# Row maxima of attention scores: five two-bank reduces per head in place of twelve one-bank ones

## The reference

```python
k = (x @ Wk).reshape(B, H, T, hs)      # B 32, H 6, T 1024, hs 16
q = (x @ Wq).reshape(B, H, T, hs)
v = (x @ Wv).reshape(B, H, T, hs)
wei = einsum('bhtd,bhsd->bhts', q, k) * C ** -0.5
wei = where(tril(ones((T, T))), wei, -inf)
wei = softmax(wei, axis=-1)
out = einsum('bhts,bhsd->bhtd', wei, v).reshape(B, T, C)
return out @ Wp + bp
```

## Time and profile before

| | us |
|---|---|
| median of 3 runs | 2901.9 |
| lowest, highest run | 2897.7, 2904.84 |
| profiled execution, span from first to last instruction | 2901.5 |

### The profile page before, as it was taken

How to read it: one execution, slowest core, us unless ns; L and a number is a source line. 1 busy time by engine, 2 the same in 40 slices (tenths; PEclk the granted TensorE clock), 3 DMA queues, 4 the chain that set the end, 5 groups by cost and what they waited for, 6 DMA issues and landing times. The chain is left out here.

```text
span 2901.5 us, 86028 instructions
## 1 busy us (share of the span) xinstructions
PE 2730.6 (94%) x28924; PEld 1685.7 (58%) x29306; DVE 2300.3 (79%) x4585; ACT 2020.8 (70%) x3943; POOL 1153.0 (40%) x1999
## 2 busy tenths in 40 slices
PE   4999999999999499999999999999999997899996
PEld 2555555555554266666666666666666664455553
DVE  3577676676765499999999999999999994678997
ACT  2677777777776267777777777777777774577775
POOL 1144443444434434444444444444444441224445
PEclk9999999999999699999999999999999998999998
DMA  1113223232332466666666666666666663334555
GB/s 34 44 55 115 90 100 114 76 114 85 105 114 85 128 118 119 116 118 118 118 118 118 118 118 118 118 117 117 117 117 117 118 117 86 99 105 132 147 142 154
DMA packets 923408, 316.04 MB, mean 109 GB/s; under 512 B 848785, under 2 KB 906418, under 8 KB 923314
## 3 DMA queue, kind: packets, MB, share of 16 engines
q1 hardware_dynamic: 921970, 313.59, 47.8%
q10 hardware_dynamic: 1344, 1.18, 0.1%
HBM read 113.35 MB, written 99.88 MB: 73 GB/s over the span
## 5 line engine op out<-in xcount | busy, mean ns | idle before, releaser
L982 DVE TENSOR_REDUCE at_unit_max<-at_ps_queries 128x1 f32<-128x512 f32 (+4 forms) x2304 | 1135.9, 550 | 86.0 <-PE at_ps_queries L853 83.5
L928 ACT ACTIVATE at_probs<-at_ps_keys 128x512 f32<-128x512 f32 x1344 | 743.3, 603 | 388.9 <-PE at_ps_keys L868 384.5
L853 PE MATMUL at_ps_queries<-at_turned 96*128 96x128 bf16 (+3 forms) x3456 | 635.1, 275 | 30.6 <-DMA at_turned<-at_spread 29.4
L868 PE MATMUL at_ps_keys<-at_turned 128*128 128x128 bf16 x3453 | 648.4, 275 | 13.3 <-ACT at_probs L928 1.7
L803 POOL TENSOR_TENSOR at_v<-at_stacks,at_one 128x128 f32<-128x128 f32 x192 | 76.7, 399 | 818.5 <-DMA at_stacks<-qkv_rows 818.5
L888 PE MATMUL at_ps_values<-at_probs,at_v 128*32 128x128 f32 x10752 | 373.4, 276 | 6.5 <-ACT at_probs L928 6.5
L868 PEld LDWEIGHTS at_ps_keys<-at_turned 128*128 128x128 bf16 x3456 | 238.0, 97 | 239.5 <-ACT at_probs L928 88.3
L853 PEld LDWEIGHTS at_ps_queries<-at_turned 96*128 96x128 bf16 x3456 | 289.7, 98 | 122.0 <-DMA at_turned<-at_spread 31.3
L888 PEld LDWEIGHTS at_ps_values<-at_probs,at_v 128*32 128x32 f32 x10752 | 269.5, 109 | 120.6 <-ACT at_diag_probs L928 70.2
L928 ACT ACTIVATE at_diag_probs<-at_ps_keys 128x512 f32<-128x512 f32 x384 | 208.7, 595 | 8.5 <-PE at_ps_keys L868 5.6
L822 POOL TENSOR_SCALAR_AFFINE_SELECT at_diag_probs<-at_diag_probs 128x1024 f32<-128x1024 f32 x192 | 210.3, 1095 | 0.0
(11 more groups left out here) (214 smaller groups left out, 4967.4 us busy)
## 6 DMA issues: line engine op xcount, KB each, us to landing
qkv_rows<-cb_packed SPq DMA_DIRECT2D x32, 1536.0 KB, 8.3
at_stacks<-qkv_rows SPq DMA_DIRECT2D x192, 256.0 KB, 3.3
cb_x<-in_x_dram SPq DMA_DIRECT2D x32, 384.0 KB, 3.7
cb_x_again<-in_x_dram SPq DMA_DIRECT2D x32, 384.0 KB, 4.5
x_after_conv<-cb_x SPq DMA_DIRECT2D x32, 384.0 KB, 5.0
attention_rows<-at_att SPq DMA_DIRECT2D x384, 32.0 KB, 2.2
ff_att_rows<-attention_rows SPq DMA_DIRECT2D x32, 384.0 KB, 4.5
ff_x<-x_after_conv SPq DMA_DIRECT2D x128, 96.0 KB, 2.4
```

What stands on the lines that cost most here:

```text
L853: mm = pe.matmul(pq[:, u % QBANKS, c0:c0 + n], QT[0:STACK, slot, qb * P:(qb + 1) * P], KT[0:STACK, slot, k0:k0 + n], start=(c0 == 0), stop ...
L868: mm = pe.matmul(pk[:, bank_k, c0:c0 + n * P], KT[:, slot, kb * P:(kb + 1) * P], QT[:, slot, q0 * P:(q0 + n) * P], start=(c0 == 0), stop=True,
L928: act.activation(probs, pk[:, (slot * NU + k) % KBANKS, :], ACT.Exp, scale=scale).then_inc(S["probs"], 1)
L982: dve.tensor_reduce(peaks, scores, AX.X, ALU.max).then_inc(S["unit_max"], 1)
```

## The change

The query side's twelve units are regrouped into five, each over two PSUM banks (a pair), and one `tensor_reduce` of up to 1024 columns reads a whole pair. There are two pairs, so a unit waits for the reduce of the unit two earlier. The units are, in order: LOW (rows 4 and 5, keys 0 to 511), EDGE (row 3, and row 7 keys 512 to 895), DIAGONAL (the eight diagonal blocks, a mask in each bank), HIGH (rows 6 and 7, keys 0 to 511) and SHORT (rows 1, 2 and the rest of 5 and 6). They stand at steps 1, 2, 4, 6 and 8. `unit_peaks` gives each reduce its place in `MX`, which has four partial maxima per row instead of three. The turn of the maxima moves from step 2 to 3, its copy on ACT from 3 to 4, and the division of the output comes before the last reduce, as before.

```diff
--- before.py
+++ after.py
@@ -696,16 +696,21 @@
     WIDE = NU - DIAG
     SLOTS = 6
     BATCHES = {4: (0, 1, 2, 3, 4), 8: (5, 6, 7, 8)}
-    QBANKS, KBANKS = 4, 2
-    QDIAG = [[(qb, qb * P, P) for qb in range(g, g + HALF)] for g in (0, HALF)]
-    QUNITS = [[(1, 0, P)], [(2, 0, 2 * P)], QDIAG[0], [(4, 0, BANK)], [(5, 0, BANK)], [(3, 0, 3 * P)], [(6, 0, BANK)],
-              [(5, BANK, P)], QDIAG[1], [(7, BANK, 3 * P)], [(6, BANK, 2 * P)], [(7, 0, BANK)]]
+    QPAIRS, KBANKS = 2, 2
+    LOW, HIGH, EDGE, DIAGONAL, SHORT = range(5)
+    QUNITS = [[[(4, 0, BANK)], [(5, 0, BANK)]],
+              [[(6, 0, BANK)], [(7, 0, BANK)]],
+              [[(3, 0, 3 * P)], [(7, BANK, 3 * P)]],
+              [[(qb, qb * P, P) for qb in range(g, g + HALF)] for g in (0, HALF)],
+              [[(1, 0, P), (2, 0, 2 * P)], [(5, BANK, P), (6, BANK, 2 * P)]]]
+    QORDER = [LOW, EDGE, DIAGONAL, HIGH, SHORT]
     NQ = len(QUNITS)
-    QSTEP = [1, 2, 2, 3, 4, 4, 5, 6, 6, 7, 7, 8]
+    QSTEP = [1, 2, 4, 6, 8]
+    PEAKS = 4
     LAG = 11
     VALUES_LAG = 14
-    MAX_TURN, MAX_COPY, OUT_COPY, OUT_TURN = 2, 3, 5, 8
-    OUT_QUNIT = 11
+    MAX_TURN, MAX_COPY, OUT_COPY, OUT_TURN = 3, 4, 5, 8
+    OUT_QUNIT = 4
     VW = 32
     with ExitStack() as ctx:
         def sb(name, shape, dt=FP32):
@@ -726,7 +731,7 @@
         QT = TURNED[:, :, 1, :, :].rearrange("p s t n -> p s (t n)")
         A1, B1 = (sb(f"w1_{side}", [C, GROUPS * (HIDDEN // GROUPS)]) for side in ("above", "below"))
         A2, B2 = (sb(f"w2_{side}", [P, CHUNKS, GROUPS * (C // GROUPS)]) for side in ("above", "below"))
-        MX = sb("unit_max", [P, 2, TILES, 3])
+        MX = sb("unit_max", [P, 2, TILES, PEAKS])
         NM = sb("neg_max", [P, TILES])
         MP = sb("max_parts", [P, 2, P], BF16)
         MT = sb("max_rows", [2 * TILES, 2, P], BF16)
@@ -737,7 +742,7 @@
         ONE = sb("one", [P, 1, 1])
         OT = sb("out_t", [P, 2 * P])
         AT = sb("att", [P, SLOTS, TILES, HD])
-        pq = pb("queries", [P, QBANKS, BANK])
+        pq = pb("queries", [P, QPAIRS, 2, BANK])
         pk = pb("keys", [P, KBANKS, BANK])
         pv = pb("values", [P, 2 * P])
         bank = pb("turn", [P, BANK])
@@ -847,15 +852,18 @@
                     slot = (r - 2) % SLOTS
                     if u == 0:
                         pe.wait_ge(turned_in[slot], _dmas(lap, r, 2, SLOTS))
-                    _above(pe.wait_ge, S["unit_max"], NQ * h + u - QBANKS + 1)
-                    c0 = 0
-                    for qb, k0, n in QUNITS[u]:
-                        mm = pe.matmul(pq[:, u % QBANKS, c0:c0 + n], QT[0:STACK, slot, qb * P:(qb + 1) * P],
-                                       KT[0:STACK, slot, k0:k0 + n], start=(c0 == 0), stop=True, skip_group_check=True)
-                        c0 += n
-                    if len(QUNITS[u]) > 1:
-                        mm = pe.matmul(pq[:, u % QBANKS, :], w["ident_bf"][:, :], w["mask_queries"][:, :],
-                                       start=False, stop=True, skip_group_check=True)
+                    _above(pe.wait_ge, S["unit_max"], NQ * h + u - QPAIRS + 1)
+                    pair = (slot * NQ + u) % QPAIRS
+                    for a, blocks in enumerate(QUNITS[QORDER[u]]):
+                        c0 = 0
+                        for qb, k0, n in blocks:
+                            mm = pe.matmul(pq[:, pair, a, c0:c0 + n], QT[0:STACK, slot, qb * P:(qb + 1) * P],
+                                           KT[0:STACK, slot, k0:k0 + n], start=(c0 == 0), stop=True,
+                                           skip_group_check=True)
+                            c0 += n
+                        if QORDER[u] == DIAGONAL:
+                            mm = pe.matmul(pq[:, pair, a, :], w["ident_bf"][:, :], w["mask_queries"][:, :],
+                                           start=False, stop=True, skip_group_check=True)
                     mm.then_inc(S["q_scores"], 1)
 
                 def key_scores(h, slot, lands, u):
@@ -961,8 +969,24 @@
                 dve.tensor_tensor(w["w1"][0:C, 0:GROUPS * gs1], A1[:, :], B1[:, :], ALU.subtract)
                 dve.tensor_tensor(w["w2"][:, :, 0:GROUPS * gs2], A2[:, :, :], B2[:, :, :], ALU.subtract)
 
+                def unit_peaks(u, half, slot):
+
+                    peaks, scores = MX[:, half, :, :], pq[:, (slot * NQ + u) % QPAIRS, :, :]
+                    unit = QORDER[u]
+                    if unit == LOW:
+                        return peaks[:, 4:6, 0], scores
+                    if unit == HIGH:
+                        return peaks[:, 6:8, 3], scores
+                    if unit == EDGE:
+                        return peaks[:, 3:8:4, 0], scores[:, :, 0:3 * P]
+                    if unit == DIAGONAL:
+                        return peaks[:, :, 2], scores.rearrange("p a (t n) -> p (a t) n", n=P)
+                    flat = peaks.rearrange("p (a t) s -> p a (t s)", a=2)
+                    return flat[:, :, 2 * PEAKS - 1:2 * PEAKS + 2], scores[:, :, 0:3 * P].rearrange(
+                        "p a (t n) -> p a t n", n=P)
+
                 def body(i, r, lap, on):
-                    for u, blocks in enumerate(QUNITS):
+                    for u in range(NQ):
                         if u == OUT_QUNIT and on(5):
                             q = (r - 5) % SLOTS
                             dve.wait_ge(S["out_turned"], i - 4)
@@ -973,12 +997,7 @@
                                               ALU.mult).then_inc(S["out_ready"], 1)
                         if on(2):
                             dve.wait_ge(S["q_scores"], NQ * (i - 2) + u + 1)
-                            qb, k0, n = blocks[0]
-                            if len(blocks) > 1:
-                                peaks, scores = MX[:, r % 2, qb:qb + len(blocks), 2], pq[:, u % QBANKS, :].rearrange(
-                                    "p (t n) -> p t n", n=P)
-                            else:
-                                peaks, scores = MX[:, r % 2, qb, k0 // BANK:k0 // BANK + 1], pq[:, u % QBANKS, 0:n]
+                            peaks, scores = unit_peaks(u, r % 2, (r - 2) % SLOTS)
                             dve.tensor_reduce(peaks, scores, AX.X, ALU.max).then_inc(S["unit_max"], 1)
                     if on(2):
                         dve.wait_ge(S["unit_max"], NQ * (i - 1))
```

## The result

The changed kernel takes 3084.6 us (median of 4 runs, 3083.1 to 3085.3) against 2900.3 for the kernel before (median of 4 runs, 2897.7 to 2904.8): ratio 1.0632, 95% interval 1.0617 to 1.0647. The forecast was 3098, with a range from 3010 to 3160. Its profiled span is 3081.4 us.

The account below looks back on a forecast made before the run. PE in its written order was taken as the bound. Four waits of 0.24 + 0.18 + 0.19 + 0.38 = 0.99 us per head (190 us) plus 8 us at the branch raised 2901.5 to 3099.5, taken as 3098; range 3010 to 3160.

Parts of the forecast that it names:

- The reduces: Row-maximum reduces on DVE: 1024 columns estimated at 1.21 us, 768 at 0.95, against 0.684 for 512.
- 5.59 less 5.13: DVE's reduce time per head in us before and after; the prediction gave the saving as 0.47, worth about nothing.
- k1: Second key unit's product on PE, forecast to wait 0.24 us per head for ACT's exponential to free its bank.
- DIAGONAL: Diagonal query scores on PE, forecast to wait 0.18 us more per head for the reduce of LOW.
- k4: Fifth key unit's product, after HIGH on PE, forecast to wait 0.19 us per head for an exponential.
- k5: Sixth key unit's product on PE, forecast to wait 0.38 us per head for an exponential.
- the row copy: ACT's copy of the row maxima, moved behind the third key unit's exponential; priced at 0.13 us, bounds 0 and 0.26.
- SP's small stores: Stores said to land in 2.0 us; the row of maxima had 4 us, so nothing was charged.
- The loop's branch: Once in six heads DVE was forecast some 0.25 us late at the branch: 0.04 per head, 8 us.
- DVE as the bound: Rival: DVE, 92% busy, bounds the attention stage, so its saved 0.47 us per head gives 2879 us; chance 4%.
- Only the pair ring costs: Rival: ACT keeps up and only the coarser query-bank ring costs: 2982 us (2940 to 3020); chance 12%.
- The clock: Rival: about 1 us of holes per head lowers PE's clock: 3120 to 3300 us, taken as 3220; chance 6%.

Follow-up runs that it names:

- the third experiment: Kernel before the change, with each reduce reading only half of its columns: 2897.0 us, ratio 0.9990 to the kernel before.
- the fourth: Changed kernel's order and steps kept, each pair taken apart into four single banks with ten one-bank reduces: 3054.6 us, ratio 1.0530 to the kernel before.
- the spread order: Changed kernel's two pairs and five reduces, units reordered and each pair's halves computed at separate steps: 2879.7 us, ratio 0.9923 to the kernel before.

## Why the prediction was right

**The bound.** DVE at 92% was not the bound of the kernel before: shown by half of the columns, where a quarter of DVE's time had no measurable price. That PE in its written order was the bound is only half of the truth. Without the masks PE's work fell by 0.44 us and the head stayed at 7.18, held by the exponentials through the two key banks. PE's products and the releases of the banks filled the head about equally, and the prediction named only the first. The forecast did not suffer from it, since the change took no work from PE.

**The reduces.** I estimated 1.21 and 0.95 us. Groups by shape of the changed kernel, 1450 to 1532 us:

```profile
L1001 DVE TENSOR_REDUCE at_unit_max<-at_ps_queries 128x8 f32<-128x1024 f32 x10 | 12.3, 1226 | 2.9 <-PE at_ps_queries L865 2.9
L1001 DVE TENSOR_REDUCE at_unit_max<-at_ps_queries 128x6 f32<-128x768 f32 x11 | 10.4, 947 | 0.0
```

By the slope of one bank (0.684 us for 512 columns and 1.036 ns for each further one) 1024 columns would take 1.21 us: two banks in one pass cost 0.01 us more at most, and the view of eight blocks takes the same 1.226 us as that of two rows. (The prediction's 5.59 less 5.13 is 0.46, not 0.47; nothing hangs on it.) The queued pair of 1024 and 768 columns takes 2.09 us together, 0.09 less than the sum of 1.23 and 0.95, so the 0.065 us for a queued reduce beside its columns held too. The 0.125 us of the Trainium skill (VectorE: DVE Perf Modes, The TRN2 errata) lie between that spacing and the duration's share: 1.226 us less 1024 columns at 0.96 GHz is 0.16.

**The four waits.** Forecast k1 0.24, DIAGONAL 0.18, k4 0.19, k5 0.38; measured 0.24, 0.19, 0.20, 0.40. The totals of the waits view I forecast badly, about 150 us for the key products and 35 for the query scores against 275.7 and 22.6, since they count idle weight loads, not late matmuls. The step with a guess in it was the row copy: 0.13 assumed, as half of another copy; 0.16 between its start and the next exponential's, and 0.13 less wait at k5 when it was put back. That a guess between 0 and 0.26 came out so close was in part luck., read as the landing of "SP's small stores", shows the stores of the output, not the row of maxima; the landing of that row was never read, and only k0's start on time shows that it did no harm.

**The loop's branch.** Here the forecast had the wrong sign: 8 us more, DVE being late behind the branch. The starts of the output copy on ACT, one per head, over six heads of the kernel before and of the changed one:

```profile
1471.51 0.39 ACT L937 ACTIVATE at_out_t<-at_ps_values 128x256 f32<-128x256 f32 x1
1479.14 0.39 ACT L937 ACTIVATE at_out_t<-at_ps_values 128x256 f32<-128x256 f32 x1
...
1508.09 0.39 ACT L937 ACTIVATE at_out_t<-at_ps_values 128x256 f32<-128x256 f32 x1
1515.27 0.39 ACT L937 ACTIVATE at_out_t<-at_ps_values 128x256 f32<-128x256 f32 x1
```

```profile
1480.29 0.36 ACT L945 ACTIVATE at_out_t<-at_ps_values 128x256 f32<-128x256 f32 x1
1488.83 0.36 ACT L945 ACTIVATE at_out_t<-at_ps_values 128x256 f32<-128x256 f32 x1
...
1521.60 0.36 ACT L945 ACTIVATE at_out_t<-at_ps_values 128x256 f32<-128x256 f32 x1
1529.77 0.36 ACT L945 ACTIVATE at_out_t<-at_ps_values 128x256 f32<-128x256 f32 x1
```

Before, six heads take 43.76 us, 7.29 each, 0.11 over the undisturbed 7.18. After, they take 49.48, 8.25 each, 0.08 over 8.17. So the branch costs about 0.04 us per head less than before, where I forecast 0.04 more; the difference is some 15 us, about what the forecast of 3098 was too high by (13 us). The undisturbed head grew by 0.99, as forecast: 190 us in 192 heads, less 7 for the branch, less 3 because the last three copies of the stage, where the pipeline drains, follow each other at 6.94, 6.75 and 4.99 us, nearly as before (6.80, 6.80, 4.99). That gives 180, and the two profiled spans differ by 3081.4 - 2901.5 = 179.9. Next to nothing is left for the other stages. The medians differ by 184; single executions of the kernel before lie up to 7 us apart.

Do the holes take up part of the branch's delay? Those for exponentials do not: with four single banks k1, k4 and k5 wait as in the changed kernel, six heads take 48.57 us against 7.99 for an undisturbed one, and the branch costs 0.11 per head, as before. In the three kernels in which DIAGONAL waits for LOW's reduce (the changed one, with the row copy back, without masks) it costs 0.07 to 0.08. That this one hole takes up the rest is my reading; no run isolates it.

**The rivals.** DVE as the bound fell with the third experiment. "Only the pair ring costs" fell with the fourth: the pairs are worth 30 us, the order of the steps 154. The clock did not fall: 1.00 granted, at 2.4 GHz, with about 1 us of holes in every head of 8.17. The Trainium skill (TensorE: Matmul & The Clock Gate, A second HAM failure mode) describes a kernel whose small idles, while cycling PSUM banks, made the clock go back and forth; this trace shows nothing of the kind.

**What was missed on the way.** For the spread order I expected a head of 7.15 to 7.18 and the branch as before. Its output copies:

```profile
1473.94 0.36 ACT L948 ACTIVATE at_out_t<-at_ps_values 128x256 f32<-128x256 f32 x1
...
1502.52 0.36 ACT L948 ACTIVATE at_out_t<-at_ps_values 128x256 f32<-128x256 f32 x1
1509.64 0.36 ACT L948 ACTIVATE at_out_t<-at_ps_values 128x256 f32<-128x256 f32 x1
1517.01 0.36 ACT L948 ACTIVATE at_out_t<-at_ps_values 128x256 f32<-128x256 f32 x1
```

An undisturbed head takes 7.12 us (1502.52 to 1509.64), 0.06 less than before. Six heads take 43.07, 7.18 each, so the branch costs 0.06 per head instead of 0.11. Together that is 0.11 us per head, 22 us in 192 heads, all that was measured; the two parts are about equal. That both shrink because this order leaves ACT room before the key products is my reading.

## What to carry to other kernels

Merging instructions on an engine for which nobody waits bought nothing here; ask first who waits for it. When instructions are grouped anew, look at what their producers stood between: here the query products were the filler that gave ScalarE time to free one of two banks, and moving them together cost some four times what the coarser ring did. And a product that seems to be pure overhead on the bounding engine (the masks) may fill a wait: lay out the head with all releases before counting its removal as gain, and reorder with it.

## What the runs showed of the hardware

A reduce that reads two PSUM banks in one pass runs at nearly the rate of one bank: 1.226 us for 1024 columns against 0.684 for 512, 1.06 ns for each further column, where it was 1.04 from 128 to 512 columns within one bank. The granted clock stayed at 1.00 through 1200 us in which PE waited about an eighth of each head, in pieces of 0.2 to 0.4 us.
